# Softmax maxima handled by eight heads instead of four, and a first pass of scores that runs 14 heads ahead

## What is computed

```python
b, s, d_model = x.shape            # 16, 256, 128
h, hd = 16, 8
scale = jnp.sqrt(jnp.float32(h + D_KV + D_Q))        # 144
query, key = qt_c + qt_r, kt_c + kt_r                # 16 heads of 8 channels
attn = jnp.einsum('bhqd,bhkd->bhqk', query, key) / scale
attn = jax.nn.softmax(attn, axis=-1)
out = jnp.einsum('bhqk,bhkd->bhqd', attn, value)
x = x + (out.transpose(0, 2, 1, 3).reshape(b, s, d_model) @ Wo_w + Wo_b)
```

## Time and profile before

| | us |
|---|---|
| median of 3 runs | 598.53 (596.14 to 602.67) |
| profiled execution, its own time | 595.82 |
| its span in the trace | 593.6 |
| TensorE busy | 512.5 (86% of the span) |
| VectorE, ScalarE, GpSimd busy | 393.1, 343.3, 345.9 |
| steps of the attention | about 34.5 to 353 |
| one step in the middle | 19.6 to 20 |

### The profile page before, as it was taken

One profiled execution on the slowest core, in us unless ns is written; L12 is line 12 of the kernel. 1 busy time (PEld: TensorE's weight loads), 2 busy tenths in 40 slices (PEclk: granted clock), 3 DMA queues, 4 the chain that ended last, 5 costly groups with the idle time before them and its releaser, 6 DMA issues.

```text
span 593.6 us, 16730 instructions
## 1 busy us (share of the span) xinstructions
PE 512.5 (86%) x4402; PEld 386.0 (65%) x4403; DVE 393.1 (66%) x1179; ACT 343.3 (58%) x881; POOL 345.9 (58%) x623
## 2 busy tenths in 40 slices
PE   7699889899899999999999887868799999999900
PEld 5566455566556655665566557867799998999800
DVE  7698678679778887887687725545455545555446
ACT  2157566677677677767665654433355545555642
POOL 6556564777667766776675454456445554555521
PEclk9999889999999999999999998898799999999965
DMA  6455455545544554455444483122332222221074
GB/s 227 143 152 159 149 153 164 150 137 154 163 127 139 150 172 138 137 168 160 132 140 137 132 260 108 51 64 74 142 77 67 61 55 56 61 62 46 1 243 181
DMA packets 66130, 75.53 MB, mean 127 GB/s; under 512 B 11874, under 2 KB 52459, under 8 KB 65696
## 3 DMA queue, kind: packets, MB, share of 16 engines
q1 hardware_dynamic: 59840, 62.13, 36.1%
q0 software_dynamic: 5152, 10.70, 5.2%
q10 hardware_dynamic: 1088, 2.10, 1.2%
HBM read 50.99 MB, written 25.08 MB: 128 GB/s over the span
## 4 chain that ended last, share of the span: by engine, by line
PE 56%; issue 9%; DVE 8%; DMA 8%; SPq 6%; POOL 5%; ACT 2%; another core or an unknown queue 2%; ACTq 1%; POOLq 0%; DVEq 0%
PE s L899 13%; PE s L907 12%; PE pv L656 7%; PE s L625 6%; PE s L644 5%; DVE mx L1118 3%; SPq L435 2%; DMA w<-mrow 2%; PE pb L681 2%; DVE w L1608 2%; PE pb L697 2%; PE pb L682 1%; DMA w<-parts_out 1%; DMA parts_out<-qkp 1%
## 5 line engine op out<-in xcount | busy, mean ns | idle before, releaser
L1118 DVE TENSOR_REDUCE mx<-s 128x2 f32<-128x512 f32 x256 | 172.6, 684 | 66.9 <-PE s L625 64.4
L938 ACT ACTIVATE pr<-s 128x512 f32<-128x512 f32 x256 | 146.4, 589 | 82.1 <-PE s L644 76.5
L1093 ACT ACTIVATE pr<-s,wts 128x128 f32<-128x128 f32 x352 | 100.7, 369 | 93.8 <-PE s L899 72.5
L1820 POOL DMA_INDIRECT results<-pr,ridx x88 | 94.0, 1068 | 87.6 <-DVE pr L1289 55.3
L644 PE MATMUL s<-w 75*128 75x256 bf16 x512 | 99.3, 275 | 9.7 <-DMA w<-mrow 5.2
L625 PE MATMUL s<-w 72*128 72x256 bf16 x512 | 99.8, 276 | 7.6 <-DVE mx L1118 4.1
L907 PE MATMUL s<-w,pr 128*128 x704 | 96.8, 282 | 10.3 <-ACT pr L1093 5.4
L907 PEld LDWEIGHTS s<-w,pr 128*128 128x128 f32 x704 | 88.7, 198 | 11.6 <-issue 11.6
L1702 POOL DMA_INDIRECT dispatched<-pay,pos x64 | 63.9, 998 | 31.6 <-issue 11.1
L625 PEld LDWEIGHTS s<-w 72*128 72x128 bf16 x512 | 40.7, 100 | 49.8 <-DVE mx L1118 29.6
L656 PE MATMUL pv<-pr,vm 128*32 128x256 f32 x1024 | 71.5, 398 | 0.5 <-ACT pr L938 0.5
(11 more groups left out here) (209 smaller groups left out, 814.8 us busy)
## 6 DMA issues: line engine op xcount, KB each, us to landing
w<-in_w SPq DMA_DIRECT2D x20, 512.0 KB, 4.0
w<-parts_out SPq DMA_DIRECT2D x32, 288.0 KB
w<-parts_out SPq DMA_DIRECT2D x96, 96.0 KB
parts_out<-qkp SPq DMA_DIRECT2D x16, 384.0 KB
tin<-dispatched SPq DMA_DIRECT2D x88, 66.0 KB
weighed_out<-weighed_sb SPq DMA_DIRECT2D x16, 256.0 KB
w<-results SPq DMA_DIRECT2D x8, 512.0 KB, 7.6
outT<-weighed_out SPq DMA_DIRECT2D x16, 128.0 KB
```

What stands on the lines that cost most here:

```text
L938: nc.scalar.activation(pr[h // NG % 2][:, h % NG, :, :], s2[h % 2][:, :, :], ACT.Exp, scale=SCALE).then_inc(exp_done, 1)
L1093: last = nc.scalar.activation(hT[t.pair][:, c, :], hps[t.pair][:, :, :].rearrange("p a s -> p (a s)")[:, c * P:(c + 1) * P], ACT.Gelu, bia ...
L1118: nc.vector.tensor_reduce(mx[j % 2][:, :, g], s1[h % 2][:, :, :], AX.X, ALU.max).then_inc(max_done, 1)
L1820: nc.gpsimd.indirect_dma_start(results, bass.IndirectOffsetOnAxis(ap=ridx[t.slot][:, 0:1], axis=0), yo[t.slot], None, bounds_check=TOPK * ...
```

## The change

Maxima are kept, split, turned, cast and sent for eight heads at a time, so there are two rounds a step instead of four, each with tiles of twice the width (GpSimd 128x16 for 128x8, the turned rows 24x256 for 12x256, the transfer 12 KB for 6 KB). Each half has tiles of its own. The lead is 14 heads: `pass1` does head h+14 of batch b in slots 0 and 1, and head h-2 of batch b+1 from slot 2 on. The second half of batch b is turned in slot 3 (needed in slot 8), the first half of batch b+1 in slot 11 (needed in slot 0 of the next step, five slots later). ScalarE casts in slots 4 and 12. On GpSimd `add_out_bias` moves behind the second split, and `deviation_rows` and `third_part` stand ahead of it. On SyncE `load_weighed` moves behind the first `spread_rows`. Ahead of step 0 there are 14 first-pass heads and one round, where there were 12 and two.

```diff
+NH = 2
+HALF = H // NH
+LEAD = 14
-        mx = [sb(f"mx{i}", [P, QT, NG]) for i in range(2)]
-        mxp = [sb(f"mxp{i}", [P, QT, NP, NG], BF16) for i in range(2)]
-        mrow = [sb(f"mrow{i}", [NP * NG, S], BF16) for i in range(2)]
+        mx = [sb(f"mx{i}", [P, QT, HALF]) for i in range(NH)]
+        mxp = [sb(f"mxp{i}", [P, QT, NP, HALF], BF16) for i in range(NH)]
+        mrow = [sb(f"mrow{i}", [NP * HALF, S], BF16) for i in range(NH)]
...
-            return (b, s, q + 3) if q < 1 else (b + 1, 1 - s, q - 1)
+            return (b, s, h + LEAD) if h < H - LEAD else (b + 1, 1 - s, h + LEAD - H)
+        TURN_SECOND, TURN_FIRST = 3, 11
...
                 if held.attend:
-                    add_maxima(*turning(b, s, 0))
+                    add_maxima(b, s, 1)
...
-                if held.attend:
-                    add_maxima(*turning(b, s, 1))
                 if held.weigh:
                     store_inverse(b - 1)
                 if held.project:
                     store_parts(b + 2)
                 if held.lead:
-                    add_maxima(*turning(b, s, 2))
+                    add_maxima(b + 1, 1 - s, 0)
+                if held.project:
+                    spread_rows(b + 2, s, 0)
                 if held.weigh:
                     load_weighed(b - 1)
-                if held.project:
-                    spread_rows(b + 2, s, 0)
-                if held.lead:
-                    add_maxima(*turning(b, s, 3))
...
-                    if g == 2 and turns(held, q):
-                        turn_max(*turning(b, s, q))
+                    if h == TURN_SECOND and held.attend:
+                        turn_max(b, 1)
+                    if h == TURN_FIRST and held.lead:
+                        turn_max(b + 1, 0)
...
-            for h in range(NG):
+            for h in range(LEAD):
                 pass1(0, 0, h)
                 keep_warm(3, pv[:, 0, :])
-            for j in range(2):
-                for g in range(NG):
-                    pass1(0, 0, NG * (j + 1) + g)
-                    keep_warm(3, pv[:, 0, :])
-                turn_max(0, 0, j)
+                if h == HALF + 2:
+                    turn_max(0, 0)
...
-            for g in range(NG):
-                maximum(0, 0, 0, g)
+            for h in range(HALF):
+                maximum(0, 0, h)
             take_rotary(2, r1_full, turn1, C_COS, r1_done, True, pb)
...
                 if held.attend:
-                    split_maxima(*turning(b, s, 0)[::2])
+                    split_maxima(b, 1)
...
                 if held.send:
                     send(b - 4, s, 1)
-                if held.attend:
-                    split_maxima(*turning(b, s, 1)[::2])
                 if held.project:
                     leave(b + 2)
-                    add_out_bias(b + 2)
-                if held.lead:
-                    split_maxima(*turning(b, s, 2)[::2])
                 if held.mix:
                     deviation_rows(b - 2)
                 if held.project:
                     third_part(b + 2)
+                if held.lead:
+                    split_maxima(b + 1, 0)
+                if held.project:
+                    add_out_bias(b + 2)
...
-                if held.lead:
-                    split_maxima(*turning(b, s, 3)[::2])
...
+            add_biases(2)
             split_maxima(0, 0)
-            add_biases(2)
-            split_maxima(0, 1)
```

More of the change, by code:

```diff
@@ L280, in build @@
         inv_st, pv_done = sem("inv_st"), sem("pv_done")
-        max_in = [sem(f"max_in{j}") for j in range(NQ)]
+        max_in = [sem(f"max_in{j}") for j in range(NH)]
         part1_done, rest_done, part2_done, part3_done = sem("part1_done"), sem("rest_done"), sem("part2_done"), sem("part3_done")
@@ L374, in __init__, with leading, leads @@
                 self.weigh, self.mix, self.route, self.send = (not known or 0 <= b - i < NB for i in (1, 2, 3, 4))
-        def leading(b, s, q):
-            return (b, s, q + 3) if q < 1 else (b + 1, 1 - s, q - 1)
[L380 to L390, removed]
+        def leading(b, s, h):
+            return (b, s, h + LEAD) if h < H - LEAD else (b + 1, 1 - s, h + LEAD - H)
+        def leads(held, h):
+            return held.attend if h < H - LEAD else held.lead
+        TURN_SECOND, TURN_FIRST = 3, 11
         block = ctx.enter_context(nc.Block())
@@ L436, in spread_rows, with add_maxima @@
                                  q.rearrange("i (d f) -> d i f", d=HD)[:, :, fs]).then_inc(spread_in[half], 16)
-            def add_maxima(m, s, j):
-                turned = known_count(sp, m * NQ + (j + 1))
+            def add_maxima(m, s, half):
+                turned = known_count(sp, m * NH + (half + 1))
                 wait(sp, mt_done, turned)
-                sp.dma_start(qrows[s][KR:KR + NP, NG * j:NG * j + NG, :], mrow[j % 2][:, :]).then_inc(max_in[j], 16)
+                sp.dma_start(qrows[s][KR:KR + NP, half * HALF:(half + 1) * HALF, :], mrow[half][:, :]).then_inc(max_in[half], 16)
             def store_weighed(b):
@@ L939, in exponents, with take_maxima @@
                                      scale=SCALE).then_inc(exp_done, 1)
[L941 to L947, removed]
+            def take_maxima(m, half):
+                wait(act, mt_full, m * NH + (half + 1))
+                wait(act, max_in[half], m * 16)
+                nc.scalar.copy(mrow[half][:, :], mturn).then_inc(mt_done, 1)
             def first_part(b):
@@ L1004, in step @@
                     q, g = divmod(h, NG)
-                    if g == 3 and turns(held, q):
-                        m, _, j = turning(b, s, q)
-                        take_maxima(m, j)
+                    if h == TURN_SECOND + 1 and held.attend:
+                        take_maxima(b, 1)
+                    if h == TURN_FIRST + 1 and held.lead:
+                        take_maxima(b + 1, 0)
                     if held.attend:
@@ L1057, in _ @@
             take_maxima(0, 0)
-            take_maxima(0, 1)
             pipeline(act, step)
@@ L1112, in _, with maximum @@
         def _(dve):
-            def maximum(m, s, j, g):
-                h = NG * j + g
+            def maximum(m, s, h):
+                half, g = divmod(h, HALF)
                 wait(dve, s1_full, m * H + (h + 1))
                 if g == 0:
-                    wait(dve, split_done, m * NQ + (j - 1))
-                nc.vector.tensor_reduce(mx[j % 2][:, :, g], s1[h % 2][:, :, :], AX.X, ALU.max).then_inc(max_done, 1)
+                    wait(dve, split_done, m * NH + (half - 1))
+                nc.vector.tensor_reduce(mx[half][:, :, g], s1[h % 2][:, :, :], AX.X, ALU.max).then_inc(max_done, 1)
             def stats_x(first, last):
@@ L1362, in step @@
                         stats_x(m * QT, (m + 1) * QT)
-                    if leads(held, q):
-                        m, ms, j = leading(b, s, q)
-                        maximum(m, ms, j, g)
+                    if leads(held, h):
+                        maximum(*leading(b, s, h))
                     if held.project:
@@ L1452, in _ @@
             nc.vector.tensor_copy(rk[1][:, QT, :], consts[:, C_BASE:C_BASE + NE]).then_inc(rank_done, 1)
-            for g in range(NG):
-                maximum(0, 0, 0, g)
+            for h in range(HALF):
+                maximum(0, 0, h)
             take_rotary(2, r1_full, turn1, C_COS, r1_done, True, pb)
             dve.wait_ge(ld_x, 32)
-            for j in range(1, NQ - 1):
-                for g in range(NG):
-                    maximum(0, 0, j, g)
+            for h in range(HALF, LEAD):
+                maximum(0, 0, h)
             pipeline(dve, step)
```

37 lines of the change are left out of this document (16 added, 21 removed).

## The result

| | kernel before | changed kernel |
|---|---|---|
| median | 598.4 us (596.14 to 602.67, 4 runs) | 608.81 us (607.49 to 612.2, 4 runs) |
| ratio | 1 | 1.0176 (95%: 1.0133 to 1.0219) |
| span of the profiled execution | 593.6 us | 608.0 us |
| mean granted clock | 0.949 | 0.930 |
| last copy of weighed values out of PSUM (end of the attention phase) | 354.33 | 364.42 |

The change made the kernel slower by 1.8%; 597 was forecast, with 606 as the upper end. Of the 14.4 us between the two spans 10.1 had arisen by the end of the attention phase.

The account below looks back on a forecast made before the run. TensorE's in-order stream and its waits were taken as the bound. Terms +2.3 - 1.4 + 10 x 0 - 0.5 - 1.6 = -1.2 took 595.8 to 594.6; the median's 2.7 more gave 597 us, range 588 to 606.

Parts of the forecast that it names:

- Spread rows, needed two slots earlier: First-half spread rows, read in slot 2 instead of 4, would land in time by 0.2 us; 0.1 us a step allowed.
- rival two: Spread rows come late at pass1 of slot 2: 0.9 us a step, +9 in ten steps, 606 us; chance 0.19.
- The other steps: Steps 0 to 3 gain, mostly from shorter waits for maxima rows: 0.5 us for step 0, 0.3 each for 1 to 3.
- Ahead of step 0: Eight maxima instead of four before the first split: the second pass starts at 37.0 instead of 34.68, +2.3 us.
- GpSimd's order and the turn in slot 11: TensorE waits 0.7 to 0.95 us for the split behind third_part, ScalarE's 0.37 wait goes; net -0.05 a step.
- the ends of -0.9 and +1.0: Bounds in us on the change of a middle step, whose forecast value was 0.
- The turn in slot 3: The second half's turn, needing head 15 from slot 1, priced at nothing; 0.3 us a step if its thin cover goes.
- The end: Step 14, without third_part, gains 0.5 us; the last step gains 1.4 from two leading maxima and 0.2 from a turn.
- The rules weighed: For SyncE's merged maxima transfer, coalescing would make steps 1 to 3 gain; the engine limit would lose a little.

Follow-up runs that it names:

- after_again: The changed kernel as it is, run again for comparison in a later group of runs; ratio 1.0167 to the kernel before.
- store_first: The changed kernel with the store of the parts put ahead of the store of the inverse on SyncE; ratio 0.9948 to the kernel before, repeated at 0.9939.
- store_split: The changed kernel with the store of the parts first on SyncE, and the next batch's first-half split ahead of third_part on GpSimd; ratio 1.0816 to the kernel before.

## Why the prediction was wrong, step by step

**The failed step is "Spread rows, needed two slots earlier".** It priced the wait at 0.1 us a step, with an issue at 250.5, 0.8 behind the rows of maxima, and "their stores landed by then". The store had not landed. It took 2.73 us in most steps and 4.5 in step 2, and went out behind the store of the inverse; the spread rows followed 1.54 behind the maxima. The landing after the first issue, taken as 6, was 6.4 in after_again (239.31 to 245.68). Late by 0.7 and longer by 0.4, against a margin of 0.2: that is rival two, with its place and its feeding on itself as written.

Its number, 606, where 0.19 of the chance lay, came near for other reasons than its own. It had 0.9 us in each of ten middle steps. In the changed kernel's first trace steps 5 to 14 were 0.2 longer each, with waits for spread rows of 0.5 at most up to step 13. The time went in steps 2 to 5, which rival two did not price, ahead of step 0, and for 4.3 of the 14.4 us in the phase of tiles. That part is luck.

The prediction had what it needed. In the kernel before, `load_weighed` stood in front of the spread rows, which in a middle step went out 3.57 us behind the store (248.72 and 252.29 in the earlier trace rows), later than its landing. The change took `load_weighed` away, and the landing came to the front. And in steps 0 and 1, where less time lay between the two, the chain of the kernel before does show the landing, with 2.75 and 2.73 us. In step 1:

```profile
67.18 2.73 DMA parts_out<-qkp
...
69.93 0.84 SPq L431
```

I took a time that nothing had waited for in a middle step as covered. store_first and its repetition support the chain as the cause: it was shortened, and the loss was gone. They are not a full proof, since the same swap costs time at lead 13, and that is unexplained.

**"The other steps"**: -0.3 for each of steps 1 to 3. The waits of the earlier trace rows did shrink as forecast. But steps 2 to 5 cost 5.9 us more, from the stands of 2.56, 1.41 and 1.52 (at 102.08, 124.90 and 147.35) and the lower clock behind those at 78.22, 102.08 and 124.90. Behind the one at 147.35 it stayed at 1.00. The forecast had no term for the clock, and the earlier trace rows had been read for eight middle steps only.

**Ahead of step 0**: +2.3 forecast, +3.7 measured (38.41 for 34.68). The split ended at 35.30 for 34.5, and issue to landing took 2.3 for 1.8. By step 1 it was +4.2, where 1.8 had been forecast.

**GpSimd's order and the turn in slot 11** was right in size: 0.87 us in most middle steps (0.7 to 0.95 forecast), and ScalarE's wait gone. Middle steps 5 to 14 came out 0.2 us longer each (1.5 + 0.8 - 0.5 over nine), within the ends of -0.9 and +1.0.

**The turn in slot 3** waited 0.48 us in step 0 (at 41.77) and 1.23 in the last step (at 348.19), and in no middle step: nothing, as priced. **The end** was right: -1.6 from step 14 on for -2.1.

**The rules weighed.** Waits for rows of maxima fell from 5.2 us (4 times) before to 1.7 (2 times). That is the direction in which the Trainium skill (DMA: Bandwidth & Descriptors, Rules for kernel authors) has coalescing of small transfers; the opposite loss, from three rows as outermost dimension, does not show. No run here varies the size alone.

## What to carry to other kernels

Before an operand's first use is moved forward, list the whole chain behind it, stores, landings and what stands ahead of them in the queue, and close it over one step: if the ring is as long as the step, a saving on the busiest engine is worth nothing, and a delay in it costs every step. What stands in front of a transfer can hide a landing, so taking it away brings the landing out. A transfer that nobody waits for shows no landing time in the profile; that is no sign of a short one, and another step, in which something did wait, may show it. And when a step sits between two rings of nearly one length (19.6 and 19.5 us here), mend the one that the chain names and profile again before the next edit: the swap of two transfers gave 2.3% (1.0167 to 0.9939), and of the five further edits on top of it four lost and the fifth gave nothing.

## What the runs showed of the hardware that was not expected

- A stand can cost more than it lasts, but its length does not tell. Behind stands of 1.55, 1.67 and 2.83 us the granted clock was about 0.5 for 3.4 to 7 us; behind the 0.87 us at the turn it stayed at 1.00, but also behind 1.82 and 1.75 us in after_again (147.10 and 167.32) and 2.42 in store_split (83.54).
- One packet of 16 KB of instruction code, 0.95 us long, held up the end of a 384 KB store: 4.4 to 4.7 us to the issue behind it in step 2 in four executions, for 2.7 to 2.8 in middle steps. The order of this store and the one of 16 KB beside it changes nothing in middle steps.
- TensorE's results reached two idle engines over 2 us after its passes had started, beside an indirect send.
- The same kernel took 573 us in two groups of runs and 595 to 598 in others. The phase of tiles took 217 to 224 us in the first two groups and 238 to 244 in the rest, whatever the kernel. The groups ran on three chips, but one chip (number 9) gave both 573 and 595, so it is not the chip alone.
